# Experts' products handed out in pairs by the number of a tile's passes, their first weights brought from device memory

## The reference

```python
for i in range(3):
    h = (x @ W[i]).reshape(N, 8, 32)
    e = leaky_relu(el[src] + er[dst]);  a = softmax of e over each dst
    x = segment_sum(h[src] * a, dst) + b[i]          # leaky_relu after layers 0 and 1
x = x0 + that + linear_attention(x0n)
xn = layernorm(x) * gamma + beta
w_full = softmax of the two largest of xn @ Wr + br, zero elsewhere
for e in range(8):
    y += (gelu(xn @ W1[e] + b1[e]) @ W2[e] + b2[e]) * w_full[..., e]
out = x + y
```

## Time and profile before

| | |
|---|---|
| median of 3 runs | 7141.27 us (7137.47 to 7150.18) |
| the profiled execution | 7151.61 us |
| its span, first to last instruction | 7149.9 us |
| mean granted clock of TensorE | 0.895 |
| TensorE busy | 5616.7 us, 79% |
| GpSimd busy | 4535.0 us, 63% |
| VectorE busy | 4514.0 us, 63% |
| ScalarE busy | 1582.9 us, 22% |

### The profile page before, as it was taken

How to read it: one execution, slowest core, us unless ns; L and a number is a source line. 1 busy time by engine, 2 the same in 40 slices (tenths; PEclk the granted TensorE clock), 3 DMA queues, 4 the chain that set the end, 5 groups by cost and what they waited for, 6 DMA issues and landing times.

```text
span 7149.9 us, 149324 instructions
## 1 busy us (share of the span) xinstructions
PE 5616.7 (79%) x35000; PEld 4505.8 (63%) x35001; DVE 4514.0 (63%) x11249; ACT 1582.9 (22%) x4666; POOL 4535.0 (63%) x4739
## 2 busy tenths in 40 slices
PE   4687777777776777777777777999999988888767
PEld 2566656555554666555555556888888777776546
DVE  5677766666555667766665556555666666667664
ACT  2111111000000000000000004555555444433212
POOL 0677777777776677777777775344444455666774
PEclk9788888888877888888888778999999999999989
DMA  4555555555554445455554443222223333444442
GB/s 170 180 148 151 152 150 153 149 145 146 145 142 130 135 140 149 143 146 148 145 145 142 141 133 100 74 78 80 84 84 90 92 95 102 115 118 129 138 134 84
DMA packets 386097, 916.19 MB, mean 128 GB/s; under 512 B 130561, under 2 KB 192777, under 8 KB 385930
## 3 DMA queue, kind: packets, MB, share of 16 engines
q0 software_dynamic: 227904, 681.63, 34.8%
q1 hardware_dynamic: 115530, 194.09, 8.2%
q10 hardware_dynamic: 42624, 40.02, 1.7%
HBM read 871.89 MB, written 43.49 MB: 128 GB/s over the span
## 4 chain that ended last, share of the span: by engine, by line
PE 30%; POOL 27%; issue 23%; DVEq 7%; DVE 6%; DMA 2%; ACTq 2%; ACT 2%; POOLq 1%; SPq 0%
POOL gat L434 27%; PE bank L1516 11%; PE bank L1428 7%; PE looked_up L1439 5%; PE bank L1439 5%; DVEq L265 2%; DMA gat<-table,meta 2%; ACTq L265 1%; DVE sel L1176 1%; PE bank L1382 1%; DVE selT L1133 1%; ACT L524 1%; DVEq L1176 1%; DVE lg L1156 1%; DVEq L1156 1%
## 5 line engine op out<-in xcount | busy, mean ns | idle before, releaser
L434 POOL DMA_INDIRECT gat<-table,meta x4716 | 4521.7, 959 | 2477.3 <-issue 1363.9
L1516 PE MATMUL bank<-msg,sel 128*128 x10536 | 3192.0, 454 | 919.9 <-DVE sel L1176 902.8
L1516 PEld LDWEIGHTS bank<-msg,sel 128*128 128x128 f32 x10536 | 2187.7, 218 | 1380.0 <-issue 1002.2
L1166 DVE SCALAR_TENSOR_TENSOR msg<-bank,gat 128x1056 f32 x1317 | 1654.0, 1256 | 263.6 <-ACT bank L568 250.8
L568 ACT ACTIVATE bank<-lg 128x32 f32<-128x32 f32 x1317 | 262.0, 199 | 4556.4 <-DVE lg L1160 4402.3
L1176 DVE TENSOR_TENSOR sel<-iota_t,meta 128x256 f32<-128x256 f32 x2634 | 1004.2, 419 | 45.3 <-PE bank L1516 38.2
L1482 PEld LDWEIGHTS looked_up<-uvb,selT 128*128 (+1 forms) x10584 | 485.5, 99 | 685.0 <-issue 601.7
L1482 PE MATMUL looked_up<-uvb,selT 128*128 (+1 forms) x10584 | 543.0, 173 | 395.5 <-DVE selT L1133 385.3
L1156 DVE TENSOR_TENSOR lg<-gat,looked_up 128x64 f32 x878 | 193.3, 220 | 960.4 <-POOLq L441 787.1
L1428 PEld LDWEIGHTS bank<-xT,w 128*128 128x128 f32 x6272 | 750.5, 192 | 15.8
L1428 PE MATMUL bank<-xT,w 128*128 128x128 f32 x6272 | 759.6, 276 | 0.0
(11 more groups left out here) (231 smaller groups left out, 2821.3 us busy)
## 6 DMA issues: line engine op xcount, KB each, us to landing
dstb<-dst_lists SPq DMA_DIRECT2D x297, 512.0 KB
gat<-table,meta POOLq DMA_INDIRECT x4716
table<-hrow ACTq DMA_DIRECT2D x98, 140.0 KB
w<-in_W SPq DMA_DIRECT2D x2, 4096.0 KB
table<-hrow SPq DMA_DIRECT2D x49, 140.0 KB, 1.8
region<-xnT_d ACTq DMA_DIRECT2D x50, 128.0 KB
region<-qT_d ACTq DMA_DIRECT2D x50, 128.0 KB
res<-in_x SPq DMA_DIRECT2D x1, 6272.0 KB, 25.3
```

Source lines behind the costliest of these rows:

```text
L434: pool.indirect_dma_start(gat[:, r, c, :], None, table[l], bass.IndirectOffsetOnAxis(meta[:, m, c, 0:1].bitcast(U32), 0)).then_inc(s_done, 16)
L1166: dve_v.scalar_tensor_tensor(msg[:, bass.ds(n % 2, 1), :, :].rearrange("p a c (h d) -> p (a c) h d", h=H), ex_p.unsqueeze(3).to_broadcast( ...
L1516: last = pe.matmul(acc[:, 0:MSG], sel[:, c, :], msg[:, bass.ds(m % 2, 1), c, :].rearrange("p a m -> p (a m)"), start=opens and c == 0, sto ...
```

## The change

The unit of work is now a pair of experts, `k` = 0 to 195, four pairs a tile, numbered through all tiles.

* At the start, three control values more are computed for each tile from the passes up to it: the pairs are handed out in proportion to the passes (184 over all passes, at least 0.41 a pass), within two limits: no pair of a tile before its features and weights exist, and none more than 14 tiles behind. `tile_groups` reads five values: pairs `k0` to `k1` are done ahead of the tile's passes, pairs `k1` to `k2` in trips, each of two passes and a pair, and the passes that are left follow alone.
* A tile's pairs can come up to 16 tiles later, so that its features are also copied to a ring of 16 (`xT_kept`), and its routing weights to `shares`.
* W1 is no longer held in SBUF. Each expert's part (512 KB) is brought from device memory to one of two fixed places (`stage`) by a DMA on ScalarE's queue, which is issued ahead of the Gelu of the pair before.
* `take_out` adds a result to `res` itself, one pair later than it is made; b2's term is added by `add_bias`; SyncE stores the tiles behind the last list that it loads.
* The first pair that ends up behind the last pass is 183; 13 pairs are done there.

```diff
-CTL = 11
+CTL = 16
+PAIRS = 4
+KEPT = 16
+LAG = 3
+SPARE = 2
+OFFSET = 1024
+GROUPS = PAIRS * NT
+LOOPED = PAIRS * (NT - 2) - 1
...
-        w1 = sb("w1", [P, EXPERTS, 2, HID])
+        stage_rows = sb("stage_rows", [P, 2, 2, HID])
+        stage = tuple(stage_rows[:, j, :, :] for j in range(2))
+        xT_kept = sb("xT_kept", [P, KEPT, 2, P])
+        shares = sb("shares", [P, NT * EXPERTS])
...
+            row = ctl[0:1, bass.ds(T, 1), 11:16].rearrange("a b c -> a (b c)")
+            _, values = nc.values_load_multi_w_load_instructions(row, engines=[eng.engine], min_val=1, max_val=TOTAL_MAX)
...
-                    for dst, src in ((w1[:, :, :, :], a["W1"].rearrange("e (k p) h -> p e k h", p=P)),
-                                     (w2[:, :, :, :], a["W2"].rearrange("e (k p) c -> p e k c", p=P)),
+                    for dst, src in ((w2[:, :, :, :], a["W2"].rearrange("e (k p) c -> p e k c", p=P)),
...
+            with sp.Fori(0, NT) as T:
+                at = sp.snap(T * -1 + (NT - 1))
+                rows = sp.snap(T * -P + (NT - 1) * P)
+                sp.wait_ge(f_yd, EXPERTS * T + EXPERTS + 2)
+                sp.sem_inc(turn_taken, 1)
+                sp.dma_start(out[bass.ds(rows, P), :], res[:, bass.ds(at, 1), :].rearrange("p a c -> p (a c)")).then_inc(f_out, 16)
...
+            def load_stage(k, j):
+
+                expert = (2 * k + j) % EXPERTS
+                act.dma_start(stage[j], w1_rows[:, bass.ds(expert, 1), :, :].rearrange("p e k h -> p (e k) h")
+                              ).then_inc(stage_in[j], 16)
...
+            def gelu(k, j, load=True):
...
+                act.wait_ge(f_h, 2 * k + (j + 1 + UP_TO))
+                if load:
+                    act.sem_inc(turn_taken, 1)
+                    load_stage(k + 1, j)
+                for b in range(HB):
+                    last = act.activation(gT[:, j, b, :], bank[5 + j][:, b * P:(b + 1) * P], ACT.Gelu,
+                                          bias=b1[:, bass.ds(expert * HB + b, 1)])
...
+                act.wait_ge(f_h, EXPERTS * (T + 1))
+                act.sem_inc(turn_taken, 1)
+                for c in range(2):
+                    act.activation(xT_kept[:, bass.ds(T % KEPT, 1), c, :].rearrange("p a n -> p (a n)"), tp[:, c * P:(c + 1) * P], ACT.Identity,
+                                   bias=gb[:, 2 + c:3 + c], scale=gb[:, c:c + 1])
...
+                def last_tile(T, expert, following):
+
+                    shift, first, _, _, last, _ = tile_slots(act, T)
+                    grouped = not isinstance(T, int) or T >= LAG
+                    if grouped:
+                        k0, k1, k2, begin, at = tile_groups(act, T)
+                        if isinstance(T, int):
+                            group(0)
+                        with act.Fori(k0, k1) as k:
+                            group(k)
+                        warm_exp()
+                    else:
+                        begin = act.snap(first + 1)
+                    weigh(act.snap(first + shift))
+                    weigh(act.snap(first + shift + 1))
+                    if expert is not None:
+                        router_tanh(expert)
+                    if following is not None:
+                        deviation(following)
+                    if grouped:
+                        with act.Fori(k1, k2) as k:
+                            group(k)
+                            warm_exp()
+                            n = act.snap((2 * k + at) % OFFSET + shift)
+                            weigh(act.snap(n + 1))
+                            weigh(act.snap(n + 2))
+                    else:
+                        warm_exp()
+                    if expert is not None:
+                        weights_copy(expert)
+                    with act.Fori(begin + 1, last + 1) as g:
+                        weigh(act.snap(g + shift))
+                    if following is not None:
                         to_features(following)
...
+                    load_stage(0, 0)
+                    load_stage(0, 1)
...
+            dve_v.tensor_scalar(share_of, share_of, float(LOOPED - PAIRS + 1), 0.41, ALU.mult, ALU.max)
...
+            dve_v.tensor_scalar(ismall[0:NT, 8:10], counted, share_of, None, ALU.mult)
...
+            dve_v.tensor_tensor(groups, groups, limit, ALU.min)
...
+            dve_v.scalar_tensor_tensor(groups, limit, float(-PAIRS * (KEPT - SPARE)), groups, ALU.add, ALU.max)
...
+            dve_v.scalar_tensor_tensor(trips, trips, -1.0, passes, ALU.add, ALU.min)
...
+            def take_out(k, j):
+
+                unit = within(2 * k + (j - 2), EXPERTS * NT - 1)
+                rows = res_tile(unit // EXPERTS)
+                dve.wait_ge(f_y, 2 * k + (j + 1))
+                dve.sem_inc(turn_taken, 1)
+                dve_v.scalar_tensor_tensor(rows, y_psum[j][:, 0:C], shares[:, bass.ds(unit, 1)], rows, ALU.mult, ALU.add).then_inc(f_yd, 1)
...
+                    if grouped:
+                        k0, k1, k2, begin, at = tile_groups(dve, T)
+                        with dve.Fori(k0, k1) as k:
+                            group_out(k)
...
+                    end1, end2, last, g_next, unshared = tile_slots(dve, T, (5, 10))
+                    dve.drain()
+                    if following is not None:
+                        dve.sem_inc(turn_taken, 1)
+                        with dve.Fori(unshared, first + 2):
+                            dve.sem_inc(slot_done[l], 1)
+                        activate(following)
+                    else:
+                        dve.sem_inc(slot_done[l], 1)
+                    if expert is not None:
+                        largest_two(expert)
...
+                    if grouped:
+                        with dve.Fori(k1, k2) as k:
+                            g = dve.snap((2 * k + at) % OFFSET)
+                            one_pass(g)
+                            take_out(k, 0)
+                            one_pass(dve.snap(g + 1))
+                            take_out(k, 1)
+                    else:
+                        one_pass(begin)
+                        begin = dve.snap(begin + 1)
+                    if expert is not None:
+                        weights(expert)
+                    if following is not None:
+                        normalise(following)
...
+                    if expert is not None:
+                        add_bias(expert)
...
+            def up(k, j):
+
+                pe.wait_ge(stage_in[j], 16 * k + 16)
+                pe.sem_inc(turn_taken, 1)
...
+                        last = pe.matmul(bank[5 + j][:, b * P:(b + 1) * P], stage[j][:, c, b * P:(b + 1) * P],
+                                         kept[:, c, :], start=(c == 0), stop=(c == 1))
...
+                pe.wait_ge(f_g, 2 * k + (j + 1))
+                pe.wait_ge(f_yd, 2 * k + (j + 1))
...
+                    last = pe.matmul(y_psum[j][:, 0:C], gT[:, j, b, :], w2[:, bass.ds(expert, 1), b, :].rearrange("p a c -> p (a c)"),
+                                     start=(b == 0), stop=(b == HB - 1))
...
+            def half_group(k, j, following=True):
+
+                down(k, j)
+                if following:
+                    up(k + 1 if isinstance(k, int) else pe.snap(k + 1), j)
...
+                    if grouped:
+                        k0, k1, k2, begin, at = tile_groups(pe, T)
+                        begin = pe.snap(begin + AHEAD)
+                        if isinstance(T, int):
+                            up(0, 0)
+                            up(0, 1)
+                            group(0)
+                        with pe.Fori(k0, k1) as k:
+                            group(k)
...
+                    if expert is not None:
+                        route(expert)
+                    prepare_next(n0, T)
+                    pe.wait_ge(acc_free[l], T + 1)
+                    aggregate(n0, tile_first[l], T + 1, opens=True)
...
+                    if grouped:
+                        with pe.Fori(k1, k2) as k:
+                            m = pe.snap((2 * k + at) % OFFSET + AHEAD)
+                            one_pass(m)
+                            half_group(k, 0)
+                            one_pass(pe.snap(m + 1))
+                            half_group(k, 1)
+                    if expert is not None:
+                        turn_weights(expert)
+                    with pe.Fori(begin, m3) as m:
...
+                    if expert is not None:
+                        bias(expert)
+                    if following is not None:
+                        turn_next(following)
+                    n3 = pe.snap(m3 + shift)
+                    prepare_next(n3, T + 1)
+                    aggregate(n3, tile_last[l], T + 1, closes=True)
...
+                    route(NT - 2)
+                    _, _, begun, _, _ = tile_groups(pe, NT - 1)
+                    with pe.Fori(begun, LOOPED) as k:
+                        group(k)
+                    turn_weights(NT - 2)
+                    bias(NT - 2)
```

(1 more changed line is left out.)

329 lines of the change are left out of this document (173 added, 156 removed).

## The result

The changed kernel takes 7535.6 us (7532.5 to 7541.4, four runs) against 7140.2 us for the kernel before on the same chip. The ratio is 1.0552, its 95% interval 1.0534 to 1.0570. The prediction was 7570 us. The profiled execution has a span of 7535.1 us.

What follows compares the result with a forecast made beforehand. TensorE was taken to bound tiles 3 to 45 before, waits on ScalarE and VectorE chains after. Layer 2 summed to 3198 against 2841 us (+357), clock +70: +427 on 7141.3 gave 7570 us, 8-in-10 range 7230 to 7800.

Steps and rivals of the forecast that it cites:

- second idle stretch: TensorE idles 5.6 us ahead of a tile's second aggregation, while VectorE reads five values and makes the second selection.
- The walk: Step-by-step timing of a five-pass tile from D, the last selection's end in the tile before, at full clock: 41.4 us.
- the front: Tile start: TensorE idles 7.8 us until ScalarE's copies, control reads, table and Gelu allow the first down at D+9.6.
- rival of short idle stretches: Front costs nothing and the second pass comes at once: tile 28 us, total 6880 us, faster; chance 0.15.
- Five further values at 2.3 us: ScalarE's front reads five control values after the first six (3.1 us); no row showed them, 2.3 us taken in proportion.
- Further front pairs: 14 pairs ahead of tiles beyond one per tile, at TensorE's 7.0 us each: 98 us.
- A further trip: Each further trip of two passes and a pair is a cycle over three engines: 11.3 us, 76 of them 859 us.
- a lone pass: A pass standing alone is bound by VectorE: 3.4 us, 42 further ones 143 us.
- The end: Behind the last pass: 10 us until the first down, 13 pairs at 7.0, 4 for last product and store: 105 us.
- Weights: Loads of 0.5 MB land after about 4 us, before up needs them (5.9 us in trips, 5.2 in pairs without passes): hidden.
- The clock: TensorE resumes at 1.2 GHz behind idle stretches: 0 to 4.6 us a tile, 1.5 taken, +70 us.
- The table switches: ScalarE's table loads counted at 1.28 us; the page's 1.38 us drain behind each, some 470 us more, was left out.

Runs made afterwards that it cites:

- e2: Changed kernel with the Gelu of a tile's first pair done by ScalarE at the end of the tile before: 7441.3 us, ratio 1.0406.
- e3: Changed kernel with the pairs in front of a tile done behind its first pass on all three engines: 7506.2 us, ratio 1.0500.
- e1: Changed kernel with ScalarE's two reads of control values moved ahead of the four feature copies: 7486.5 us, ratio 1.0475.
- e9: Changed kernel with further front pairs behind the first exponential on ScalarE, their take-outs behind VectorE's first selection: 7508.7 us, ratio 1.0512.
- e4: Changed kernel with each weight load after the first two cut to 1/16 (32 KB), output wrong: 7544.2 us, ratio 1.0551.
- e5: Changed kernel with 35 matmuls adding zeros behind the first aggregation of every tile from 3 on: 7515.8 us, ratio 1.0527.
- e11: Changed kernel with first Gelu and take-out a tile earlier, one eight-value read per engine in front, further front pairs later: 7288.8 us, ratio 1.0212.
- e12: e11 with VectorE's later read of two values merged into its first, ten values in one: 7307.9 us, ratio 1.0235.

## Why the prediction was right

*What bounds the tile.* Right in the chain and in the tile's length, wrong in the size of the second idle stretch, and incomplete in cause. Predicted for a tile with one pair in front: 7.8 and 5.6 us idle, a tile of 41.4 us plus 1.5 for the clock. Measured: 7.4 and 2.4, a tile of 40.4 to 40.8; the 5.60 us of tile 17 agree only by chance, as that tile has two pairs. The walk can be laid beside tile 18, with D at 5121.97, the end of the selection at 5121.22. The first down starts at D+9.3 (D+9.6 predicted), the second pass's scores at D+20.6 (D+21.2), and the second aggregation at D+24.0 (D+24.5), so that the chain over ScalarE and VectorE is as walked. But the walk gave TensorE full clock, and the front pair takes 9.5 us instead of 7.0: TensorE reaches the stretch 2.4 us later and waits that much less in it. VectorE's chain hardly notices (it waits 0.16 us for the router in this tile), so that the tile's length came out in spite of it.

For the front the prediction followed one chain, the copies, reads, table and Gelu of ScalarE. The runs show three side by side: ScalarE's 7.4 us, VectorE's reads and take-out (5.24 left in e2), TensorE's own reads (4.84 in e3), which the walk left out. That changes nothing in the sum, because the longest sets it. It does change the rival of short idle stretches: had its step been right on ScalarE alone, it would have given 2.1 us a tile, not 7.8.

*Five further values at 2.3 us.* They are the five that `tile_groups` reads (the list of the change speaks of three control values more; the table has five columns more). Predicted for the two reads together: 3.1 + 2.3 = 5.4, and 0.8 for the load's issue. The 5.18 us of the changed kernel hold that issue too, and a part of the reads lies under the copies; e1, where neither is so, has 5.87 us for the reads alone. So the reads were somewhat longer than predicted, and their overlap with the copies, which the walk did not have, made up for it.

*Further front pairs.* This term was mis-sized: 7.0 us predicted, 11.2 measured (tile 7 with 51.6 against tile 6 with 40.4), 14 x 4.2 = 59 us missing. The step that failed is that a further pair costs TensorE's time alone. VectorE takes results out ahead of the first scores and so waits for the pair before; e9 got about half of the difference back: 3.3 to 4.0 of the 4.2 us in tiles with two pairs in front, 2.3 us for each further pair in those with three, less some 0.4 us that each of the late tiles became longer.

*A further trip* 11.3, measured 11.20; *a lone pass* 3.4, measured 43.8 - 40.4 = 3.4. *The last tile* 315, measured 311.5. *Tiles 0 to 2* 78, and 11 for the pair that opens tile 3; the stretch of 94.4 us holds both and the first of tile 3's pairs.

*The end.* 105 predicted, 123.6 measured. TensorE's waits there, order of time:

```profile
7426.36 3.73 PE L1582 MATMUL bank<-w,region 128*128 x8 [12.64 <-DVE res L1090]
...
7462.17 3.75 PE L1582 MATMUL bank<-w,region 128*128 128x256 f32 x8 [2.83 <-ACT region L568]
```

The first down starts 14.9 us into the stretch, not 10. The pairs take 7.0 to 7.4 us where TensorE runs at full clock, but three waits stand between them (2.83, 1.64 and 1.35 us), and behind the first wait and two of these the first down takes 3.5 to 3.8 us instead of 1.9.

*Weights.* Landing after 4.0 us, predicted about 4; hidden, as e4 shows.

*The clock.* The mechanism is there: 0.89 in tiles 3 to 45, as TensorE resumes at half clock behind each stretch. What it costs stays open: the second aggregations 18 to some 50 us by e5, the front pairs under 4 us in the tiles with one, the rest not separated; +70 is not refuted by that, but no run shows it. TensorE: Matmul & The Clock Gate of the Trainium skill (The HAM clock gate) says that idle stretches throttle the clock, and the rows agree: a down takes 3.78 us behind 7.39 us of idle time and 1.89 later. In the front of a tile with one pair what bounds the stretch is another engine, and the half clock is all but free.

*The table switches.* The Gelu follows its 1.28 us table directly (5128.49 to 5129.79). The drain of 1.38 us that ScalarE: Activation LUTs of the Trainium skill (What ACT_TABLE_LOAD costs) puts behind it shows in no row here, and the sum came out without its 470 us.

*The sum.* Layer 2 was predicted at 3198 + 70 = 3268 us and took 3232.8. Further pairs (+59) and the end (+19) came on top; against them stand the 46 tiles, 2.3 us each shorter with the clock's part than the walk (-106). Two errors of the size of 1% cancelled in part: that the total came within 0.5% is luck, the range is not. In layers 0 and 1 nothing to speak of was predicted, and the 7 us are scatter.

## What to carry to other kernels

An idle stretch has a releaser in the trace, and behind it may stand others that end a little earlier. Before pricing a wait at its length, read what each other engine does in the same stretch, sequencers too; here three chains of 7.4, 5.2 and 4.8 us lay on top of one another, and removing the longest was worth 2.1. A spread of work pays where it fills idle time; here it also left serial work of three engines with too little beside it in every one of 46 tiles. Before, TensorE was busy 40.7 of 41.4 us in such a tile, and that work lay beside its products. And control values are not free: at about half a microsecond each, with their check, eight values on every engine are a visible part of a tile of 40 us.

## What the runs showed of the hardware

*A control value costs twice.* Beside the load, each value is followed by two instructions, shown here for e11 (the same view, 360 = 45 x 8):

```profile
L289 DVEq FUSED_REGOPS  x360: 183/183/217, 4413.8 to 6850.9; - x180
L289 DVEq SEQ_ASSERT  x360: 23/23/33, 4414.0 to 6851.1; - x180
```

In the chain of the changed kernel the pairs of instructions start at 5093.26, 5093.54 and 5093.82, which with the gaps is 0.28 us a value on VectorE, on top of 0.22 for its load.

*Where the values lie matters.* The least of eight values is 0.56 to 0.61 us, the median 1.77 to 1.94. The rows of the table in e11 are 19 values of 4 bytes long and the read starts at column 11, counted from 0, so that it starts at a multiple of 16 bytes in every fourth tile: in tiles 7, 11, 15 and so on, and these are the short ones (605 to 612 ns in VectorE's tiles 7, 11, 15, 19, 23 and 27, 1844 to 1873 in the others from 4 to 29). In e12 the rows are 84 bytes long, which moves the multiple of 16 to tiles 5, 9, 13 and 17, and there ScalarE's read takes 567 to 576 ns and 1762 to 1807 in the others from 4 to 18. VectorE's "issue" ahead of the first scores of tile 15, whose read starts at byte 1184 = 74 x 16, order of time:

```profile
4901.03 0.36 DVE L1252 TENSOR_REDUCE lg<-looked_up 128x64 f32<-128x192 f32 x1 [3.62 <-issue]
...
4938.37 0.36 DVE L1252 TENSOR_REDUCE lg<-looked_up 128x64 f32<-128x192 f32 x1 [4.86 <-issue]
```

The second row is tile 16, whose read starts at byte 1260. In the changed kernel the rows are 64 bytes long and the reads start at columns 3 and 11, so that none starts at a multiple of 16; ScalarE's read of six values takes 1334 to 1377 ns in each of 45 tiles, while in the kernel before, with rows of 44 bytes, it takes 747 at the least and 1335 in the median. A table whose reads all start at a multiple of 16 bytes was not run. An estimate from these rows: 1.2 us less for a read of eight values on each engine. How much of it the tile would keep is open.
